# A two-layer model kernel on one core: the gate's gelu in the second feed-forward part as one ScalarE evaluation and one product

## The reference, cut to what matters

```python
def _L1_ffn_ref(x, gate_W_packed, gate_scales, up_W_packed, up_scales, down_W_packed, down_scales):
    ...                                      # 4096 hidden units; weights are 4-bit codes times scales
    gate = jnp.einsum('th,nh->tn', xt, Wg)
    up = jnp.einsum('th,nh->tn', xt, Wu)
    gelu = jnp.tanh(0.7978845608028654 * (gate + 0.044715 * gate ** 3)) * gate * 0.5 + gate * 0.5
    inter = gelu * up
    out = jnp.einsum('tn,hn->th', inter, Wd)
```

## Time and profile before

| | |
|---|---|
| median of 3 runs | 3091.93 us (3090.06 to 3092.86) |
| profiled execution: span from the first to the last instruction | 3094.5 us |
| PE busy | 3033.3 us (98%) |
| DVE busy | 2004.3 us (65%) |
| ACT busy | 1650.4 us (53%) |
| POOL busy | 1407.9 us (45%) |
| mean granted TensorE clock | 0.993 |

### The profile page before, as it was taken

The page is one execution under the profiler, slowest core; times in us unless marked ns, Lnnn a source line. Parts: engine busy times, 40 slices in busy tenths (PEclk is TensorE's granted clock), DMA queues, the critical chain, the costliest instruction groups (busy, mean ns, idle before and its releaser), DMA issues. The chain is left out here.

```text
span 3094.5 us, 61556 instructions
## 1 busy us (share of the span) xinstructions
PE 3033.3 (98%) x23896; PEld 2512.4 (81%) x23896; DVE 2004.3 (65%) x3562; ACT 1650.4 (53%) x4011; POOL 1407.9 (45%) x2351
## 2 busy tenths in 40 slices
PE   8999989999999999999999899999999999999999
PEld 7888867888888888888888678788888888888887
DVE  6112267787888887877788534746666666666666
ACT  5221357777788887878887633443333333222222
POOL 2322336666667666666667444323333223222212
PEclk9999999999999999999999899999999999999999
DMA  3100121111111111111121165211011101000004
GB/s 94 31 21 28 59 67 41 48 56 53 51 47 50 50 56 56 56 50 49 47 56 46 50 194 164 85 31 31 28 32 44 35 31 31 21 24 25 27 16 163
DMA packets 130243, 165.69 MB, mean 54 GB/s; under 512 B 9936, under 2 KB 72144, under 8 KB 129920
## 3 DMA queue, kind: packets, MB, share of 16 engines
q1 hardware_dynamic: 120592, 144.49, 15.2%
q10 hardware_dynamic: 9296, 17.04, 1.5%
q0 software_dynamic: 64, 0.23, 0.0%
HBM read 127.91 MB, written 33.82 MB: 52 GB/s over the span
## 5 line engine op out<-in xcount | busy, mean ns | idle before, releaser
L1489 DVE SCALAR_TENSOR_TENSOR b_zt<-b_rx,b_cw,b_zt 128x512 f32<-128x512 f32 x576 | 471.8, 819 | 22.0 <-POOL b_rx L1698 3.2
L70 PE MATMUL bank<-b_XH,b_wh 128*128 128x512 f32 x1024 | 456.9, 446 | 8.5 <-ACT b_zt L1238 7.0
L72 PE MATMUL bank<-b_XH,b_wl 128*128 128x512 f32 x1024 | 403.4, 394 | 0.0
L71 PE MATMUL bank<-b_XL,b_wh 128*128 128x512 f32 x1024 | 402.8, 393 | 0.0
L70 PE MATMUL bank<-b_XH,b_qh 128*128 128x512 f32 x1024 | 399.4, 390 | 1.4 <-DVE b_g L2654 1.4
L72 PE MATMUL bank<-b_XH,b_ql 128*128 128x512 f32 x1024 | 398.8, 389 | 0.0
L71 PE MATMUL bank<-b_XL,b_qh 128*128 128x512 f32 x1024 | 398.8, 389 | 0.0
L2764 POOL TENSOR_TENSOR b_QHL<-b_qhd,b_QHH 128x512 fp32r<-128x512 f32 x124 | 176.5, 1427 | 453.9 <-ACT b_QHH L2532 451.5
L1744 POOL TENSOR_TENSOR b_PR<-b_A,b_T 128x15 f32<-128x15 f32 (+7 forms) x480 | 168.6, 351 | 173.3 <-issue 138.5
L2532 ACT CAST b_QHH<-b_qhd 128x512 fp32r<-128x512 f32 x124 | 76.9, 622 | 294.0 <-PE bank L72 177.0
L72 PEld LDWEIGHTS bank<-b_XH,b_wl 128*128 128x128 f32 x1024 | 193.0, 188 | 44.5
(11 more groups left out here) (270 smaller groups left out, 7649.6 us busy)
## 6 DMA issues: line engine op xcount, KB each, us to landing
b_abc<-tmp_a SPq DMA_DIRECT2D x64, 256.0 KB, 3.4
b_gbc<-tmp_g SPq DMA_DIRECT2D x64, 256.0 KB, 3.8
tmp_og<-b_gg SPq DMA_DIRECT2D x64, 256.0 KB, 2.4
b_mo<-tmp_og SPq DMA_DIRECT2D x64, 256.0 KB, 3.2
b_wr<-in_Wk SPq DMA_DIRECT2D x16, 256.0 KB, 3.1
b_wr<-in_Wq SPq DMA_DIRECT2D x16, 256.0 KB, 4.2
b_wr<-in_Wv SPq DMA_DIRECT2D x16, 256.0 KB, 2.7
b_wr<-in_Wg SPq DMA_DIRECT2D x16, 256.0 KB, 4.0
```

The lines of the kernel that those rows point to most:

```text
L70: e.do.matmul(out, wh, xh, start=first and k == 0, stop=False)
L71: e.do.matmul(out, wh, xl, start=False, stop=False)
L72: m = e.do.matmul(out, wl, xh, start=False, stop=last and k == n - 1)
L1489: e.do.scalar_tensor_tensor(out=z[:, :], in0=rx[:, j:j + 512], scalar=cw[:, u // 2, KIND[name[0]], j:j + 1], in1=z[:, :], op0=ALU.mult, op ...
```

## The change

ACT evaluates the function Gelu_apprx_tanh of the gate straight from its PSUM bank into `g2`, and DVE multiplies it by up into `qhd`. The square, the tanh and two of the three DVE operations of a step are gone, with the semaphore sq1 and the factor 0.5. The wait on PE for a gate bank is now for ACT's evaluation (th1), and for an up bank for the only DVE operation (hid, now one count a step). ACT's evaluation waits for the product of two steps before.

```diff
--- before.py
+++ after.py
@@ -2405,9 +2405,9 @@
         if B_BEFORE[what]:
             p, j, i = B_BEFORE[what]
             if p == "gate":
-                e.wait_ge("hid", 3 * step_at(j, i) + 2)
+                e.wait_ge("th1", step_at(j, i) + 1)
             if p == "up":
-                e.wait_ge("hid", 3 * step_at(j, i) + 3)
+                e.wait_ge("hid", step_at(j, i) + 1)
             if p == "down":
                 e.wait_ge("ac" if j else "ac0", max(down_at(j) - 16, 0) + i + 1)
             if p == "rate":
@@ -2515,14 +2515,12 @@
         b = step_at(j, g)
         s = t["g2"][b % 2]
         e.wait_ge("gu1", 2 * b + 1)
-        e.wait_ge("hid", 3 * (b - 2) + 3)
-        e.do.activation(s[:, :], out(("gate", j, g)), ACT.Square).then_inc(S["sq1"], 1)
-        e.wait_ge("hid", 3 * b + 1)
-        e.do.activation(s[:, :], s[:, :], ACT.Tanh, scale=0.7978845608028654 * 0.044715).then_inc(S["th1"], 1)
+        e.wait_ge("hid", b - 1)
+        e.do.activation(s[:, :], out(("gate", j, g)), ACT.Gelu_apprx_tanh).then_inc(S["th1"], 1)
 
     def cut(j, g):
         b, (s2, n) = step_at(j, g), divmod(g, 4)
-        e.wait_ge("hid", 3 * b + 3)
+        e.wait_ge("hid", b + 1)
         if rows_kept(j, n):
             e.wait_ge("s1", 128)
             e.do.copy(t["LHH"][2 * s2 + n - 2][:, :], t["qhd"][b % 3][:, :]).then_inc(S["hh1"], 1)
@@ -2647,15 +2645,11 @@
 
     def hidden(j, g):
         i = step_at(j, g)
-        s, h, k1, k2 = t["g2"][i % 2], t["qhd"][i % 3], out(("gate", j, g)), out(("up", j, g))
-        e.wait_ge("sq1", i + 1)
-        e.do.scalar_tensor_tensor(out=s[:, :], in0=s[:, :], scalar=1.0 / 0.044715, in1=k1, op0=ALU.add, op1=ALU.mult).then_inc(S["hid"], 1)
+        s, h, k2 = t["g2"][i % 2], t["qhd"][i % 3], out(("up", j, g))
         e.wait_ge("th1", i + 1)
-        e.do.scalar_tensor_tensor(out=s[:, :], in0=s[:, :], scalar=1.0, in1=k1, op0=ALU.add, op1=ALU.mult).then_inc(S["hid"], 1)
-        e.wait_ge("hid", 3 * i + 2)
         e.wait_ge("gu1", 2 * i + 2)
         e.wait_ge("hl1", i - 2)
-        e.do.scalar_tensor_tensor(out=h[:, :], in0=s[:, :], scalar=0.5, in1=k2, op0=ALU.mult, op1=ALU.mult).then_inc(S["hid"], 1)
+        e.do.tensor_tensor(h[:, :], s[:, :], k2, ALU.mult).then_inc(S["hid"], 1)
 
     def add(j, i):
         o, n = down_order(j)[i]
```

## The result

The changed kernel takes 3083.94 us (median of 8 runs, 3082.36 to 3085.17), the kernel before 3092.48 in the same measurement (8 runs, 3090.06 to 3096.46). The ratio is 0.997, with a 95% interval of 0.9962 to 0.9979: 8.5 us less. Forecast was 3083.3, range 3081.0 to 3089.5.

What follows compares the result with a forecast made beforehand. PE, busy for 3033.3 us, was taken as the bound, so only its waits counted. Entry 4.6 plus blocks 4.0 gave 8.6 us, taken off the median 3091.93: 3083.3, range 3081.0 to 3089.5.

Steps and rivals of the forecast that it cites:

- the three places where PE stood still: PE's waits in ffn1: entry 5.4 us, block 2's third gate half 1.7, down products at 2626 2.3; at most 9.4.
- Evaluation: ACT's gelu straight from PSUM, each step: 0.6 us taken, from 591 ns (the square) to 1.22 us (square and tanh together).
- Step 0 passes on 0.76 of 2.0: ffn1's entry: 2.0 us leave the chain, but row tile 12's copy must await PE's transposes, so only 0.76 comes through.
- Steps 1 and 2, 3.86 to 2.61: ffn1's entry, roots' end to qhd's end: 1.25 us less in each step, 3.25 in all with step 0's part.
- The entry's sum: Start of ffn1: 5.4 us lost there, less 0.6 of remaining wait and 0.2, so 4.6 gained.
- The blocks: Waits at the starts of blocks 2 and 9 go: 1.7 + 2.3 = 4.0 us gained.
- The room before block 2's gate bank: Chain through block 1 to block 2's gate bank: 6.7 us less against 1.6 missing, leaving 5.1 in hand.
- Only the blocks' waits go: Rival: PE and the row tiles set the entry's time, so gain 4.0 us, 3087.9; chance 0.19.
- A switch costs more than its row: Rival: gelu set switches cost x over 1.28 us; gain gone at x = 3.2, 3103 at x = 5; chance 0.04.
- the drain of 1380 ns: Skill's added price per switch: entry gives 1.8 us, whole sum 5.8, time 3086.1; chance 0.03.
- The evaluation is slow: Rival: ACT's evaluation takes 1.2 us, entry gains 3.4, sum 7.4, time 3084.5; included in the forecast's 0.66.
- The waits are absent in the timed runs: Rival: timed runs, unlike the profiled one, hardly have these PE waits; time about 3091; chance 0.08.

Runs made afterwards that it cites:

- three DVE operations: Changed kernel with two more DVE operations of the old shape ahead of each step's product, gelu not computed; 3090.8 us, ratio 0.9996 against before.
- the kernel with the blocks alone: Kernel before with the new step form in blocks 1 to 15 and the old form in block 0; 3088.0 us, ratio 0.9989 against before.
- The kernel with 4.6 us more in the chain: Changed kernel with two pairs of one-element sqrt and exp on ACT ahead of decays in blocks 1 to 8; 3083.6 us, ratio 0.9968 against before.
- its own experiment: Changed kernel with ACT evaluating each gate half's gelu twice, DVE and PE waiting for the second; 3086.9 us, ratio 0.9984 against before.
- four pairs of switches: Changed kernel with four pairs of one-element sqrt and exp on ACT ahead of decays in blocks 1 to 8; 3124.8 us, ratio 1.0101 against before.
- entry only: Kernel before with the new step form in block 0 and the old form in blocks 1 to 15; 3090.6 us, ratio 0.9996 against before.

## Why the prediction was right, and where it was not

**The method.** Only the three places where PE stood still behind the changed instructions counted. 175 us of work on DVE and 70 on ACT were forecast to go and to be worth nothing by themselves; 160.5 and 64.9 went over the whole span, and 8.4 came through. The forecast had 8.6. DVE's missing part is mostly a matter of counting: its 232 sums take 687 ns each in place of 683, but since fewer of them run into one another their busy time is 159.0 in place of 150.1.

```profile
L2659 DVE TENSOR_TENSOR b_QACC<-b_QACC,bank 128x512 f32<-128x512 f32 x232 | 159.0, 687 | 148.5 <-PE bank L72 148.3
```

**Evaluation.** Taken as 0.6, bounds 0.59 to 1.22; measured 0.595. That it would come out by the row with the same source and shape was right. The Trainium skill's formula in "ScalarE: Activation LUTs", section "What ACT_TABLE_LOAD costs", gives an estimate of 613 ns for 512 elements, 3% more.

**Step 0 passes on 0.76 of 2.0.** ACT's copy of row tile 12 was to start at 1988.45. It starts at 1984.35, with 4.07 that is 1988.42, and it waited for PE:

```profile
1984.35 0.59 ACT L1981 COPY b_mxr<-bank 128x512 f32<-128x512 f32 x1 [1.22 <-PE bank L1947]
...
1987.68 0.48 ACT L1988 ACTIVATE b_nsd<-b_nmv,b_eps 128x1 f32<-128x1 f32 x2
1988.18 1.28 ACT L2519 ACT_TABLE_LOAD   x1
1989.47 0.60 ACT L2519 ACTIVATE b_g<-bank 128x512 f32<-128x512 f32 x1
```

**Steps 1 and 2, 3.86 to 2.61.** The roots end at 1988.16 and the product on DVE at 1990.10 + 0.69 = 1990.79: 2.63.

```profile
1990.10 0.69 DVE L2652 TENSOR_TENSOR b_qhd<-b_g,bank 128x512 f32<-128x512 f32 x1 [3.16 <-ACT b_g L2519]
...
1997.10 0.69 DVE L2652 TENSOR_TENSOR b_qhd<-b_g,bank 128x512 f32<-128x512 f32 x1 [2.39 <-ACT b_g L2519]
...
2000.02 1.27 DVE L2060 TENSOR_TENSOR b_XL<-bank,b_XH 128x512 fp32r<-128x512 f32 x2
```

Step 2 has the same form seven microseconds later, and b_XL comes at 2000.02 + 4.07 = 2004.09, forecast 2004.06. PE's transposes of tile 14 come at 2004.91, forecast 2004.9, and the wait is 0.55, forecast 0.6.

**The entry's sum.** The fifth matmul behind the transposes of tile 14, where the slow restart ended before, starts at 2011.50 - 1979.62 = 31.88 us from the first one of ffn1 before, and at 2002.92 - 1975.55 = 27.37 after. That is 4.5 gained; forecast 4.6.

Of this, 1.6 us in the forecast's sum are the slow restart of the kernel before, and there was luck in it. It stood in both traces with the old entry (behind waits of 2.68 and 2.69 us), but a wait of 2.87 in the kernel with three DVE operations had none, so another execution of the kernel before may lack it. The interval of the timed gain, some 6.5 to 11.8 us, is too wide to tell.

**The blocks.** 8.4 - 4.5 = 3.9 gained; forecast 4.0, and 4.0 behind the entry in the kernel with the blocks alone. The room before block 2's gate bank was to be 5.1. ACT and PE there:

```profile
2104.45 1.05 ACT L2307 CAST b_qh<-b_wf 128x1024 fp32r<-128x1024 f32 x1 [5.40 <-DVE b_wf L2288]
2105.41 0.59 ACT L2519 ACTIVATE b_g<-bank 128x512 f32<-128x512 f32 x1
```

```profile
2110.59 0.39 PE L72 MATMUL bank<-b_XH,b_l1wl 128*128 128x512 f32 x1
2110.82 0.39 PE L70 MATMUL bank<-b_XH,b_qh 128*128 128x512 f32 x1
```

The evaluation frees the bank at 2106.0, and PE goes on at 2110.82 without a wait: 4.8. The kernel with 4.6 us more in the chain has no wait, and that with 10.7 more waits.

**The rivals.** *Only the blocks' waits go* is refuted by the entry alone: up to the fifth matmul behind the transposes it gained 4.5 in both kernels that change only the entry. *A switch costs more than its row* is refuted: all loads take 1283 ns, and where nothing else holds it the load starts 0.02 us behind the function ahead and the next function 0.01 to 0.02 us behind the load. That also speaks against the drain of 1380 ns which the Trainium skill adds in "ScalarE: Activation LUTs", section "What ACT_TABLE_LOAD costs": its sum was 3086.1, measured was 3083.9, and the entry would have given 1.8 instead of 4.5. *The evaluation is slow* is refuted by 595 ns; by its own experiment it would have cost 2.7, not the 1.2 that I gave it. *The waits are absent in the timed runs* is refuted by the ratio. The 2.6 us that this rival leaned on compared a span with a time. In the runs of the kernel before that list both, the span is some 1.8 us shorter than the time, so the profiled execution was about 4.4 us above the median. As far as the traces tell these lay ahead of ffn1: the first matmul of ffn1 came between 1974.11 and 1979.62 in ten executions, and before's was the latest. To take the gain off the median was right; off the span it would have been 3085.9.

**What failed.** No term of the sum, but one reason in it, and the price of one rival. I expected the remaining 0.6 us of wait to leave the clock alone because "only behind the one of 2.68" a matmul took 0.78, as if the length of the wait decided. It doesn't: 1.81 had a slow restart, 2.82 and 2.87 had none. The forecast came out since a wait of 0.55 had none; but for an evaluation of 1.2 us the same reasoning was short by 1.5. The dear switch was priced too low: for 10 us more in each chain I counted new waits in two blocks, 9.8, but the kernel with 10.7 us more has waits in all the blocks from 1 to 8 and lost 39.4. And of each block's chain I had followed the gate's arm alone; the weights' low part is a second one, for which PE waited first, with 10.7 us more, in four of the eight blocks.

## What to carry to other kernels

Where one engine is busy for 98%, list its waits behind the changed instructions, take each at its full cost on that engine's timeline (start to start, with the restart), and shorten the chain in front of it one list position at a time: 225 us of removed work were worth 8.4 here, and the sum was good to 0.2. Before a function from a new set goes into one part of a program, ask which set it leaves in force for the next part: a load of 1.28 us that nothing covered took 1.4 of the 4.5 us that the entry had gained. To compare two traces, put the zero at the last common instruction ahead of the change, since what is ahead scatters by more (5.5 us here) than many a change is worth.

## What the runs showed of the hardware

**A slow restart doesn't follow from the wait's length alone.** In ffn1 slow restarts came behind PE's waits of 1.81, 2.48, 2.51, 2.68, 2.93 and 3.27 us, and none behind 1.41, 2.01, 2.46, 2.50, 2.82 and 2.87. In mix0 the wait of 2.88 for b_mol had one in all nine traces that have this wait. In the kernel with four pairs of switches two waits of one kind, at the same place of two blocks, went both ways:

```profile
2266.03 0.79 PE L70 MATMUL bank<-b_XH,b_qh 128*128 128x512 f32 x1 [2.48 <-ACT b_g L2519]
```

```profile
2342.73 0.50 PE L70 MATMUL bank<-b_XH,b_qh 128*128 128x512 f32 x1 [2.50 <-ACT b_g L2519]
```

The windows of 4 us there: length, busy time (count) of PE, PEld, DVE, ACT and POOL, then the granted clock, the DMA share and GB/s.

```profile
2266.00:2270.00 4.00, 3.97 (x11) 3.15 (x12) 3.58 (x7) 1.62 (x3) 0.00 (x0) 0.60 0.56 133
```

```profile
2342.00:2346.00 4.00, 3.27 (x14) 2.73 (x15) 3.40 (x6) 2.32 (x5) 0.00 (x0) 1.00 0.30 66
```

A clock of 1.00 is the upper level, 2.4 GHz; 0.60 is mostly the lower, 1.2 GHz. Behind the wait of 2.93 the first matmul still took 0.50 and the granted clock was 1.00 from 2098 to 2102; it fell only then, to 0.58 from 2102 to 2106, when PE was at work again. A slow stretch cost 1.5 to 2.9 us. What decides between the two isn't settled; no run here was made for it.

**Gelu's set.** It serves tanh, square and the casts too. In block 1 ACT evaluates at 2105.41, runs two tanh of L2548 at 2105.90 and 2106.47, and evaluates again at 2107.04, with no load between. In entry only a gelu at 2020.82 is followed by a cast at 2029.86, a square at 2030.82 and a tanh at 2032.80, with no load between either. The exp of the decays and the roots need one.
